# A graph layer on one core: self-edges moved out of the count windows, degrees through DRAM, fewer products for folded biases, one load for two registers

## The reference

```python
    edge_index = jnp.stack([src, dst])
    xn = _layernorm(x, axis=-1)
    x = x + _L0_gnn_ref(xn, edge_index, W, b) + _L0_mix_ref(xn[None], Wq, bq, ..., P)[0]
    x = x + _L0_ffn_ref(_layernorm(x)[None], Wg, Wu, Wd, Wr, temperature)[0]
...
    # graph part
    ei = jnp.concatenate([edge_index, jnp.stack([self_idx, self_idx])], axis=1)
    row, col = (ei[0], ei[1])
    h = jnp.einsum('nd,od->no', x, W) + b
    deg = zeros.at[row].add(1.0)
    norm = deg[row] ** -0.5 * deg[col] ** -0.5
    out = segment_sum(norm[:, None] * h[col], row)
...
    # linear attention, 16 heads
    kv = einsum(k_prime, v); attn = einsum(q_prime, kv); return attn @ Wo.T + bo
```

## Time and profile before

| | us |
|---|---|
| median of 3 runs | 1120.11 (1119.9 to 1120.98) |
| the profiled execution | 1121.14 |
| its span, first to last instruction | 1119.2 |
| TensorE busy | 1098.6 (98%) |
| weight loads busy | 911.8 |
| VectorE / ScalarE / GpSimd busy | 369.6 / 252.9 / 287.5 |
| mean granted clock of TensorE | 0.997 |

### The profile page before, as it was taken

How to read it: one execution, slowest core, us unless ns; L and a number is a source line. 1 busy time by engine, 2 the same in 40 slices (tenths; PEclk the granted TensorE clock), 3 DMA queues, 4 the chain that set the end, 5 groups by cost and what they waited for, 6 DMA issues and landing times.

```text
span 1119.2 us, 15481 instructions
## 1 busy us (share of the span) xinstructions
PE 1098.6 (98%) x5707; PEld 911.8 (81%) x5707; DVE 369.6 (33%) x991; ACT 252.9 (23%) x398; POOL 287.5 (26%) x232
## 2 busy tenths in 40 slices
PE   5999999999999999999999999999999999999998
PEld 4888778877878888888878888887888888888887
DVE  6854665665623111222212113344321111111111
ACT  4330211112223244311111112334121111112000
POOL 5000011121222146510034443434132223325000
PEclk9999999999999999999999999999999999999999
DMA  6303011222223497704079987775022222216321
GB/s 242 114 29 104 13 29 54 62 61 64 67 91 105 153 306 243 246 1 151 28 193 325 308 242 209 223 225 146 1 86 61 61 61 61 71 52 216 105 102 66
DMA packets 144518, 139.29 MB, mean 124 GB/s; under 512 B 6636, under 2 KB 114492, under 8 KB 144189
## 3 DMA queue, kind: packets, MB, share of 16 engines
q1 hardware_dynamic: 143868, 136.20, 39.0%
q10 hardware_dynamic: 576, 2.10, 0.5%
HBM read 102.32 MB, written 35.96 MB: 124 GB/s over the span
## 4 chain that ended last, share of the span: by engine, by line
PE 97%; DVE 1%; ACT 1%; DMA 1%; issue 0%; POOL 0%; DVEq 0%
PE ps L1549 10%; PE ps L1551 10%; PE ps L1550 10%; PE ps L1817 7%; PE ps L1819 6%; PE ps L1818 6%; PE ps L1759 4%; PE ps L1753 4%; PE ps L1676 3%; PE ps L1677 3%; PE ps L1678 3%; PE ps L1733 3%; PE ps L1865 3%; PE ps L1735 3%; PE ps L1734 3%; PE ps L1864 3%
## 5 line engine op out<-in xcount | busy, mean ns | idle before, releaser
L1549 PE MATMUL ps<-w_hi,xnH 128*128 128x512 f32 x480 | 191.4, 399 | 0.2 <-POOL w_lo L686 0.2
L1550 PE MATMUL ps<-w_lo,xnH 128*128 128x512 f32 x480 | 187.3, 390 | 0.0
L1551 PE MATMUL ps<-w_hi,xnL 128*128 128x512 f32 x480 | 187.2, 390 | 0.0
L1549 PEld LDWEIGHTS ps<-w_hi,xnH 128*128 128x128 f32 x480 | 90.3, 188 | 19.8 <-POOL w_lo L686 0.7
L1551 PEld LDWEIGHTS ps<-w_hi,xnL 128*128 128x128 f32 x480 | 90.2, 188 | 19.4
L1550 PEld LDWEIGHTS ps<-w_lo,xnH 128*128 128x128 f32 x480 | 90.3, 188 | 17.6
L732 POOL TENSOR_TENSOR acc<-acc,cw 128x320 f32<-128x320 f32 x40 | 35.3, 883 | 260.9 <-ACT cw L904 260.0
L1676 PE MATMUL ps<-xnH,w_hi 128*128 128x512 f32 (+1 forms) x192 | 69.2, 360 | 0.0
L1677 PE MATMUL ps<-xnL,w_hi 128*128 128x512 f32 (+1 forms) x192 | 68.3, 356 | 0.0
L1678 PE MATMUL ps<-xnH,w_lo 128*128 128x512 f32 (+1 forms) x192 | 68.0, 354 | 0.0
L1817 PE MATMUL ps<-x2H,guH 128*128 128x512 f32 (+1 forms) x192 | 67.6, 352 | 0.4 <-ACT wT L1084 0.4
(11 more groups left out here) (313 smaller groups left out, 2058.2 us busy)
## 6 DMA issues: line engine op xcount, KB each, us to landing
cR<-c_d SPq DMA_DIRECT2D x20, 640.0 KB, 5.2
foldin<-in SPq DMA_DIRECT2D x32, 256.0 KB, 2.8
guR<-in SPq DMA_DIRECT2D x16, 512.0 KB, 5.3
c_d<-cw SPq DMA_DIRECT2D x40, 160.0 KB
w_raw<-in SPq DMA_DIRECT2D x12, 512.0 KB, 6.5
xb<-in SPq DMA_DIRECT2D x10, 512.0 KB, 4.8
qs0H<-qT_d SPq DMA_DIRECT2D x10, 512.0 KB, 5.4
qs0L<-qT_d SPq DMA_DIRECT2D x10, 512.0 KB, 6.5
```

The lines of the kernel that those rows point to most:

```text
L1549: pe.matmul(target, xnH[:, kc, cols], wH[w][:, kc, :], start=(kc == 0), stop=False)
L1550: pe.matmul(target, xnH[:, kc, cols], wL[w][:, kc, :], start=False, stop=False)
L1551: mm = pe.matmul(target, xnL[:, kc, cols], wH[w][:, kc, :], start=False, stop=(kc == KC - 1))
```

## The change

- The product with `idq` and `shifted` is gone, with its constants (`id16`, `idq`, `shifted`). The last counted product of each window closes it, after the rest loop, on TensorE and on VectorE; ScalarE waits for it through `hot_used`. The last window's share is 2 for 1, which also moves some windows between steps: the last step now closes two windows (38, 39) where it closed three (37 to 39).
- The self-edges are added when the counts are read back: GpSimd adds the identity to the diagonal block of each loaded tile (`own_edges`), and ScalarE's high part waits for it.
- `rng` holds both ends of a window side by side, and one load fills two registers.
- The degrees are one float32 product: `qmask` against `acc`, four rows of 320 in bank 6. VectorE adds 1, SyncE stores them to `deg_d` at j = 2 and reads them back as columns at j = 3. Maximum, GpSimd's maximum, root and reciprocals move from j = 1, 2, 3, 4 to j = 5, 6, 6, 8.
- The folded biases are eight products with two columns; the key bias is stored from columns, one value at a time, and VectorE's wait on that store is dropped.

```diff
-SHARE = [25, 11, 8, 7, 6, 6, 5, 5, 5, 5] + [4] * 7 + [3] * 22 + [1]
+SHARE = [25, 11, 8, 7, 6, 6, 5, 5, 5, 5] + [4] * 7 + [3] * 22 + [2]
...
-            ("rng", [1, 2, NWIN], I32), ("bvb", [P, W], F32), ("kbb", [P, W], F32), ("bkc", [P, KC], F32),
-            ("bqc", [P, KC], F32), ("acc", [P, SRCG], F32)), OP, OC)
+            ("rng", [1, NWIN, 2], I32), ("bvb", [P, W], F32), ("kbb", [P, W], F32), ("bkq", [P, 2, KC], F32),
+            ("bkf", [P, KC], F32), ("acc", [P, SRCG], F32)), OP, OC)
...
-            sp.wait_ge(bias_ev, 1)
-            sp.dma_start(fb_d[:, :], fbrow[:]).then_inc(fb_st, 16)
+            sp.wait_ge(bias_ev, 2)
+            with nc.allow_non_contiguous_dma(reason="1024 sums"):
+                sp.dma_start(fb_d.rearrange("o (c q) -> q (o c)", q=P), bkf[:]).then_inc(fb_st, 16)
             load_x(6)
             load_fold(0, 2)
             sp.wait_ge(fb_st, 16)
...
+                if j == 2:
+                    sp.wait_ge(dg, 1)
+                    sp.dma_start(deg_d.rearrange("(g c) -> g c", g=4), drow[:]).then_inc(deg_st, 16)
+                if j == 3:
+                    sp.wait_ge(deg_st, 16)
+                    with nc.allow_non_contiguous_dma(reason="1280 degrees"):
+                        sp.dma_start(dtmp[:, 0, :], deg_d.rearrange("(t q) -> q t", q=P)).then_inc(in_deg, 16)
...
-            for m, value in ((idq, 0.0), (shifted, 0.0), (acc, 0.0), (qmask, 1.0), (key1, -1.0), (key2, -1.0),
+            for m, value in ((acc, 0.0), (qmask, 1.0), (key1, -1.0), (key2, -1.0),
                              (cmin, 1000.0), (cmax, -1.0), (kvF0, 0.0), (ones8, 0.0)):
                 pool.memset(m[:], value).then_inc(consts, 1)
-            pool.wait_ge(consts, 10)
-            pool.wait_ge(ident_ok, 4)
-            pool.affine_select(out=shifted[:], in_=shifted[:], compare_op=ALU.not_equal, fill=1.0, base=SHIFT,
-                               pattern=[[-1, SHIFT + 3 * WIN + SRCG]], channel_multiplier=1).then_inc(consts, 1)
+            pool.wait_ge(consts, 8)
...
-                if j == 2:
+                if j == 6:
                     pool.wait_ge(dg_max, 1)
                     pool.partition_all_reduce(degi[:, 1:2], degi[:, 0:1], P, RMAX).then_inc(dg_max, 1)
...
+            def own_edges(i):
+                t, k = i % NT, i // NT * 2 + i % 2
+                pool.wait_ge(in_c[i % 2], 16 * (i // 2 + 1))
+                pool.tensor_tensor(cR[k][:, t, :], cR[k][:, t, :], ident[:], ALU.add).then_inc(c_own, 1)
+
             def count_low(i):
                 k = i // NT * 2 + i % 2
                 pool.wait_ge(c_hi, i + 1)
                 pool.tensor_tensor(cL[k][:], cR[k][:], cH[k][:].bitcast(F32), ALU.subtract).then_inc(c_lo, 1)
 
             add_bias(0)
+            own_edges(0)
             count_low(0)
             for i in range(2 * NT):
                 if i + 1 < 2 * NT:
+                    own_edges(i + 1)
                     add_bias(i + 1)
                     count_low(i + 1)
...
-                    for h in range(2):
-                        act.activation(fbrow[0:1, h * W:(h + 1) * W], bank(6 + h)[0:1, :], ACT.Copy)
-                    act.activation(bqf[:], bank(5, KC), ACT.Copy, scale=1.0 / HD ** 0.5).then_inc(bias_ev, 1)
+                    folded = bank(5, 2 * KC).rearrange("q (c k) -> q k c", k=2)
+                    act.activation(bkf[:], folded[:, 0, :], ACT.Copy).then_inc(bias_ev, 1)
+                    act.activation(bqf[:], folded[:, 1, :], ACT.Copy, scale=1.0 / HD ** 0.5).then_inc(bias_ev, 1)
...
-                act.wait_ge(win_mm, w + 1)
+                act.wait_ge(hot_used, SEEN[w + 1])
...
-                if j == 3:
-                    act.wait_ge(dg, 1)
+                if j == 6:
+                    act.wait_ge(in_deg, 16)
                     act.activation(dtmp[:, 1, :], dtmp[:, 0, :], ACT.Sqrt).then_inc(dg_sqrt, 1)
...
-                act.wait_ge(in_c[i % 2], 16 * (i // 2 + 1))
+                act.wait_ge(c_own, i + 1)
...
-                if t == 4:
-                    dve.wait_ge(fb_st, 16)
...
-                first = dve.value_load(rng[0:1, 0, w:w + 1], min_val=0, max_val=NCH - 1)
-                if end == SEEN[w + 1]:
-                    stop = dve.value_load(rng[0:1, 1, w:w + 1], min_val=2, max_val=NCHX - 1)
-                for n in range(begin, end):
+                dve.load(span, rng[0:1, w, :])
+                first = dve.snap(span[0], min_val=0, max_val=NCH - 1)
+                stop = dve.snap(span[1], min_val=2, max_val=NCHX - 1)
+                closes = end == SEEN[w + 1]
+
+                def counted(n):
                     if n >= RING:
                         dve.wait_ge(hot_used, n - RING + 1)
                     hot_pair(hot1[:, n % RING, :], hot2[:, n % RING, :], w, bass.ds(first + (n - SEEN[w]), 1), hot_ready)
-                if end < SEEN[w + 1]:
+
+                for n in range(begin, end - 1 if closes else end):
+                    counted(n)
+                if not closes:
                     return
                 p = w % 2
                 with dve.Fori(first + SHARE[w], stop) as j:
@@ -1277,6 +1289,7 @@
                     dve.wait_ge(rest_used[p], n + 1)
                     hot_pair(rest1[:, p, :], rest2[:, p, :], w, bass.ds(j, 1), rest_ready[p])
                     dve.reg_add(rests[p], rests[p], 1)
+                counted(end - 1)
...
-                    dve.tensor_copy(dtmp[:, 0, :], bank(6, NT)).then_inc(dg, 1)
-                    dve.tensor_reduce(degi[:, 0:1], bank(6, NT), AX_X, ALU.max).then_inc(dg_max, 1)
-                if j == 4:
+                    dve.tensor_scalar(drow[:], bank(6)[0:4, 0:SRCG], 1.0, None, ALU.add).then_inc(dg, 1)
+                if j == 5:
+                    dve.wait_ge(in_deg, 16)
+                    dve.tensor_reduce(degi[:, 0:1], dtmp[:, 0, :], AX_X, ALU.max).then_inc(dg_max, 1)
+                if j == 8:
                     dve.wait_ge(dg_sqrt, 1)
                     dve.reciprocal(dtmp[:, 2, :], dtmp[:, 1, :]).then_inc(dg, 1)
...
-                    pe.matmul(bank(6 + c // 4)[0:1, c % 4 * P:(c % 4 + 1) * P], bkc[:, c:c + 1], pbd_s[:, c, :],
-                              start=True, stop=True)
-                for c in range(KC):
-                    mm = pe.matmul(bank(5)[:, c:c + 1], pbd_s[:, c, :], bqc[:, c:c + 1], start=True, stop=True)
+                    mm = pe.matmul(bank(5)[:, 2 * c:2 * c + 2], pbd_s[:, c, :], bkq[:, :, c], start=True, stop=True)
                 mm.then_inc(bias_mm, 1)
...
-                for n in range(begin, end):
+                closes = end == SEEN[w + 1]
+                for n in range(begin, end - 1 if closes else end):
                     pe.wait_ge(hot_ready, n + 1)
                     pe.matmul(target, hot1[:, n % RING, :], hot2[:, n % RING, :], start=(n == SEEN[w]), stop=False)\
                       .then_inc(hot_used, 1)
-                if end < SEEN[w + 1]:
+                if not closes:
                     return
-                first = pe.value_load(rng[0:1, 0, w:w + 1], min_val=0, max_val=NCH - 1)
-                stop = pe.value_load(rng[0:1, 1, w:w + 1], min_val=2, max_val=NCHX - 1)
+                pe.load(span, rng[0:1, w, :])
+                first = pe.snap(span[0], min_val=0, max_val=NCH - 1)
+                stop = pe.snap(span[1], min_val=2, max_val=NCHX - 1)
                 with pe.Fori(first + SHARE[w], stop):
                     n = pe.snap(rests[p])
                     pe.wait_ge(rest_ready[p], n + 1)
                     pe.matmul(target, rest1[:, p, :], rest2[:, p, :], start=False, stop=False)\
                       .then_inc(rest_used[p], 1)
                     pe.reg_add(rests[p], rests[p], 1)
-                g, col = w // 10, SHIFT + w // 10 * WIN - w % 10 * WIN
-                pe.matmul(target, idq[:, g, :], shifted[:, col:col + SRCG], start=False, stop=True)\
-                  .then_inc(win_mm, 1)
+                pe.wait_ge(hot_ready, end)
+                pe.matmul(target, hot1[:, (end - 1) % RING, :], hot2[:, (end - 1) % RING, :], start=False, stop=True)\
+                  .then_inc(hot_used, 1)
...
-                for c in range(NT):
-                    g, col = c * P // SRCG, c * P % SRCG
-                    if col + P <= SRCG:
-                        mm = pe.matmul(bank(6)[:, c:c + 1], acc[:, col:col + P], qmask[:, g:g + 1], start=True, stop=True)
-                    else:
-                        for r, cols, q in ((0, slice(col, SRCG), g), (HD, slice(0, HD), g + 1)):
-                            mm = pe.matmul(bank(6)[r:r + HD, c:c + 1], acc[:, cols], qmask[:, q:q + 1], start=True,
-                                           stop=True)
-                mm.then_inc(deg_mm, 1)
+                pe.matmul(bank(6)[0:4, 0:SRCG], qmask[:], acc[:], start=True, stop=True).then_inc(deg_mm, 1)
```

42 lines of the change are left out of this document (20 added, 22 removed).

## The result

The kernel before took 1120.55 us in the runs beside this one (1119.9 to 1121.38), the changed kernel 1113.9 us (1112.42 to 1114.37): a ratio of 0.9941, 95% interval 0.9926 to 0.9955. It is faster by 6.65 us, where the forecast said 14.7. The profiled execution took 1114.37 us, its span is 1112.3, 6.9 less than before's.

The account below looks back on a forecast made before the run. TensorE's own work was taken as the bound (busy 1098.6 of 1119.2 us). Gains 5.36 + 0.8 + 1.53 + 1.84 + 1.74 + 3.4 = 14.7 us took the median from 1120.1 to 1105.4 us, range 1101.5 to 1111.5.

Parts of the forecast that it names:

- Folded biases: Before the window stage: eight one-row products go, gain 1.84 us; single-value store priced at 5 us (2.9 to 23), covered.
- The clock: Slow stretches at 324.5 to 328.1 and 334.5 to 338.3 us both taken as gone: 3.4 us (ends 0 and 3.4).
- a fall of the clock stays: Rival: slow stretches near 324 and 334 us don't both go; 1107.1 with one left, 1108.8 with both; 13%.
- Identity products: Window stage on TensorE: 39 products fewer at 0.1375 us each, 5.36 us; wait for the closing pair priced at nothing.
- the rival on the other side: Rival, slower: VectorE makes closing pairs late and TensorE waits, 40 x 0.62 us = 25 us, giving 1130; 4%.
- Registers and the end of the stage: Windows: one two-register load gains 0.8 us on TensorE; last kv group sooner, 1.53 us more (some 0.6 less without it).
- Degrees: Behind the window stage: one float32 product replaces 2.3 us of one-column products, gain 1.74; DRAM transfer taken at 6, no wait.
- Own edges at the read-back: Aggregation: twenty GpSimd additions at 0.45 us each (0.3 to 1.3), covered ahead of ScalarE's split; cost 0.
- Single values are slow: Rival: VectorE stands 13 us at j = 5 for the degrees' load, some 2.5 us reach TensorE: 1107.9; 3%.

Follow-up runs that it names:

- the store late: Changed kernel with the key bias's single-value store, its wait and read-back moved behind the load of the last x tile: 1107.37 us, ratio 0.9887 to before.
- the own edges alone: Kernel before with no identity products, counted closing products, last share 2 and GpSimd's additions; register loads, biases and degrees as before: 1113.86 us, ratio 0.9942.
- the biases alone: Kernel before with only the folded biases changed (products, copies and store), the store at its place: 1125.31 us, ratio 1.0043.
- the biases with the store late: Kernel before with only the folded biases changed, their store behind the load of the last x tile: 1119.06 us, ratio 0.9989.
- the registers alone: Kernel before with one load for the two registers, nothing else: 1117.65 us, ratio 0.9968.
- the degrees alone: Kernel before with only the degrees changed: one product, rows through DRAM, the maximum four tiles later: 1117.15 us, ratio 0.9967.
- the kernel with the late wait: Changed kernel, store at its place, but its wait and the read-back behind all loads of x and of the first folds: 1113.84 us, ratio 0.9937.

## Why the prediction was wrong, step by step

In the median 8.5 us are missing (1113.9 for 1105.4). With the store late 6.5 of them come back, and 2.0 don't: the first belong to the step on the folded biases, the others, as far as the runs tell, to the clock.

**Folded biases: this step failed.** The products and copies were right (-1.97 in the trace for -1.84). The store was priced at 5 us between 2.9 and 23; it took 11.15. It was still inside the ends, but the step's cover was 11.5 us for the store and a tile load together, and 11.15 and a load of 3.7 to 6.8 don't go into that: the eighth tile's statistics start at 50.95, where the forecast had 43.6. Two readings went wrong. First, the nearest row was a read into SBUF, and the store goes the other way: 1024 values are read in 2.2 us and stored in 9.8. Second, the cover was counted for SyncE's wait only, with x tile 6 left out, since it is issued ahead of the wait. But it stands behind the store in the DMA engines and lands 12.5 to 13.6 us after its issue, and VectorE had waited for it already in the kernel before (0.71 us at 39.18): it had no cover at all. Removing SyncE's wait changed nothing in the median. The stretch to the first counted product is 7.3 us longer than with the store late (77.53 for 70.21): 5.2 of it are waits, about 1.5 a fall of the clock (1.2 GHz from 61.2 to 64.2 us), and the rest is in no row. In the medians the store's place costs 6.5 us.

The Trainium skill (DMA: Bandwidth & Descriptors, Specifications) says that transfers under 512 B are done by read-modify-write. The runs don't bear out that size alone makes them dear: 128 rows of 32 bytes take 1.45 us, 1024 values 64 bytes apart 2.5 to 3.1, and the same values packed 8.7 to 9.8. The measurement decides.

**The clock: right in the trace, too large in the median.** Both falls were gone in the profiled changed kernel, and 3.1 us with them for 3.4: the own edges alone, with the degrees' products still there, have 14.99 for 18.10 in that stretch. But neither cause that the forecast named is shown. Of the fifteen profiled executions, the three whose windows, registers and degrees are those of before (the kernel before, the biases alone, the biases with the store late) have both falls, and the twelve others have neither. The own edges alone and the registers alone lost the second with the one-column products still in; the degrees alone lost the first with its idle time still in. So each of the three parts took both falls along, and why isn't shown. A third fall, near 797 us, comes and goes: six of the fifteen have it, among them the registers alone (778.3 for 776.6 in the table), and no part of the change explains it. The median run of the kernel before has a mean granted clock of 0.998 where the profiled one had 0.997, so its two falls were more than a usual run shows, and they were set off in full against the median. With the store late, the profiled execution has no fall and takes 1106.83 us with a span of 1104.8, against 1106.4 and 1104.5 in the forecast: in the trace the sum holds to 0.4 us. The median is 1107.37 for 1105.4, because the forecast kept before's 1.03 us from profile to median, while here two of the four runs have a fall (mean clock 0.998) and the median lies 0.54 above the profiled run. That both differences are the clock's is argued from the mean clocks, since only profiled executions show where a fall is. The rival "a fall of the clock stays" was the right one in kind.

The Trainium skill (TensorE: Matmul & The Clock Gate, Part 1) ties the gate to how busy TensorE has been. The changed kernel's new fall behind its idle time at 58 to 61 us agrees, and so does the one behind 3.3 us of idle time in the kernel with the late wait; the degrees alone, with 1.24 us of idle time at the last window and no fall, show that such a gap needn't bring one.

**Identity products.** 5.36 forecast, 5.33 measured alone. No wait for a closing pair, so the rival on the other side didn't come; VectorE's idle time by issue ahead of its pairs went from 36.6 to 17.0 us.

**Registers and the end of the stage.** 0.8 and 1.53 forecast, 2.43 measured with the registers alone and nothing of it with the own edges alone. The sum was right (2.33), its split wasn't: the end of the stage hung wholly on the shorter load, not to 0.6 of it.

**Degrees.** 1.74 forecast, 1.61 measured. The 1280 values came back in 3.2 us with no wait; a read, so the price of 6 was too high where that of the store was too low. GpSimd's tiles behind its later maximum cost nothing.

**Own edges at the read-back.** The additions took 0.46 us each for the 0.45 taken; behind 560 us TensorE's timeline stays the same 6.9 us ahead to the end. The additions in the changed kernel, by their tile (durations min/median/max in ns, first and last start):

```profile
L786 POOL TENSOR_TENSOR cR<-cR,ident x20: 456/461/471, 568.0 to 757.5; 128x128 f32<-128x128 f32 x20
```

**The rivals.** "Single values are slow" was held for the degrees' load alone and given 3%; the store, which had the same row and the worse direction, was left out of it, though the step named what would happen at 23 us. That is why the range stopped at 1111.5.

## What to carry to other kernels

A transfer that is issued early and waited for late isn't free: what is queued behind it in the DMA engines waits with it, so put a store of small values from many partitions that are neighbours in DRAM behind the loads that the critical path needs, not ahead of them, or leave 64 bytes between the values. When a profile has no row for a transfer, look for one in the same direction, and let the upper bound of its price into the range as a case of its own. Read a fall of the clock in one profiled execution as one draw: book it only in so far as the granted clock of the timed runs has it too.

## What the hardware showed that was not expected

- 4-byte values stored side by side from different partitions: 1.35 us for 16, 6.4 for 64, 6.7 to 7.1 for 128, 8.7 to 9.8 for 1024. With 64 bytes between them 1024 take 2.5 to 3.1 us, and 1024 are read in 2.2. While the late store was under way the DMA engines' records show no work (a share of 0.00 at 59 to 60 us).
- Loads behind the store crawl: 31 GB/s at a DMA share of 0.59, where the kernel before had 210 at 0.65. A store on ScalarE's queue holds SyncE's load back as long (13.3 us).
- One load of two registers costs about what one of a single register does: VectorE's idle time ahead of its pairs more than halved.
- Two falls of the clock (some 1.6 us each) near 324 and 334 us were in all three profiled executions without the window, register and degree parts and in none of the twelve with one of them or more. A third, near 797 us, was in six of the fifteen, without a pattern. Behind 3.3 us of idle time one lasted some 6.5 us (the kernel with the late wait), behind 2.7 us one lasted 3 (the changed kernel).
